# A later and shorter place for the routing of the last batch in a fused attention and mixture-of-experts kernel

## The reference

```python
x = x + tanh(g_xattn[0]) * _L0_xattn_ref(_layernorm(x), ctx_1024, ...)
x = x + tanh(g_ffn[0]) * _L0_ffn_ref(_layernorm(x), ...)

def _L0_ffn_ref(x, w1, b1, w2, b2, wr, br):      # x is 2048 x 256, E = 4, K = 2, H = 1024
    logits = xf @ wr + br
    topk_vals, topk_idx = jax.lax.top_k(logits, K)
    gates = jax.nn.softmax(topk_vals, axis=-1)
    h = jax.nn.gelu(jnp.einsum('nd,edh->enh', xf, w1) + b1[:, None, :], approximate=False)
    y = jnp.einsum('enh,ehd->end', h, w2) + b2[:, None, :]
    ...                                           # gated sum of the two chosen experts
```

## Time and profile before

| | |
|---|---|
| median of 3 runs | 1122.02 us (1119.51 to 1123.55) |
| the profiled execution's own time | 1117.15 us |
| its span in the profile | 1115.6 us |
| PE, DVE, ACT, POOL busy | 96%, 84%, 59%, 48% |
| expert phase in the profile | from about 855 us to the end |

### The profile page before, as it was taken

One profiled execution on the slowest core, in us unless ns is written; L12 is line 12 of the kernel. 1 busy time (PEld: TensorE's weight loads), 2 busy tenths in 40 slices (PEclk: granted clock), 3 DMA queues, 4 the chain that ended last, 5 costly groups with the idle time before them and its releaser, 6 DMA issues.

```text
span 1115.6 us, 22456 instructions
## 1 busy us (share of the span) xinstructions
PE 1067.3 (96%) x7949; PEld 710.8 (64%) x7949; DVE 942.5 (84%) x1764; ACT 655.9 (59%) x1267; POOL 534.1 (48%) x553
## 2 busy tenths in 40 slices
PE   5899999999999999999999999998999988899994
PEld 3556555655555555556555655655546988899994
DVE  7798999898889989898999898878978767676675
ACT  5555556664645765554557656544567675567662
POOL 7433475332436634342565354325851546755561
PEclk9999999999999999999999999999999999999998
DMA  7000010000000000000010000600173423565335
GB/s 205 19 11 11 20 38 11 20 11 11 11 19 26 24 11 10 20 5 26 14 31 15 10 11 11 194 11 35 54 233 140 138 82 130 179 204 173 115 118 176
DMA packets 59188, 72.04 MB, mean 65 GB/s; under 512 B 11579, under 2 KB 52167, under 8 KB 59080
## 3 DMA queue, kind: packets, MB, share of 16 engines
q1 hardware_dynamic: 54840, 61.30, 17.8%
q0 software_dynamic: 3360, 8.53, 2.0%
q10 hardware_dynamic: 880, 0.79, 0.2%
HBM read 54.84 MB, written 16.54 MB: 64 GB/s over the span
## 4 chain that ended last, share of the span: by engine, by line
PE 79%; DVE 13%; issue 3%; ACT 2%; POOL 1%; DMA 1%; SPq 0%; DVEq 0%; POOLq 0%; ACTq 0%
PE pv L1852 16%; PE sc L1836 15%; PE kv L1781 6%; PE kv L1783 5%; PE kv L1782 5%; PE sc L1781 4%; PE sc L1783 4%; PE sc L1782 4%; PE tr L1822 3%; PE mi L1781 3%; PE mi L1782 2%; PE mi L1783 2%; DVE acc L1210 2%; PE mi L1862 2%; DVE prob L1195 1%
## 5 line engine op out<-in xcount | busy, mean ns | idle before, releaser
L953 ACT ACTIVATE prob<-sc 128x1024 f32<-128x1024 f32 x256 | 249.3, 1029 | 198.4 <-PE sc L1836 196.0
L729 POOL TENSOR_TENSOR rot_s<-k_raw,sinb 128x256 f32<-128x256 f32 x128 | 109.7, 857 | 381.2 <-ACT k_raw L898 381.0
L1852 PE MATMUL pv<-prob,val 128*32 128x512 f32 x1984 | 237.8, 597 | 0.7 <-DVE recip L1229 0.7
L1195 DVE TENSOR_SCALAR prob<-prob 128x1024 f32<-128x1024 f32 x256 | 179.8, 715 | 44.6 <-ACT prob L953 42.2
L1836 PE MATMUL sc<-q_hid,w2all 64*128 64x512 f32 x1536 | 213.5, 410 | 1.2 <-DVE w2all L1175 1.2
L1836 PEld LDWEIGHTS sc<-q_hid,w2all 64*128 64x128 f32 x1536 | 135.2, 185 | 101.4 <-issue 54.2
L1210 DVE TENSOR_TENSOR acc<-acc,prob 128x1024 f32<-128x1024 f32 x120 | 177.6, 1501 | 0.0
L733 POOL TENSOR_TENSOR rot_c<-rot_c,rot_s 128x256 f32<-128x256 f32 x128 | 111.0, 867 | 34.1 <-DVE rot_c L1183 19.1
L1852 PEld LDWEIGHTS pv<-prob,val 128*32 128x32 f32 x1984 | 54.8, 109 | 106.1 <-issue 85.3
L1781 PE MATMUL kv<-w2all,acts 128*128 128x512 f32 x248 | 109.8, 443 | 2.2 <-DVE acts L1141 1.3
L1781 PE MATMUL sc<-w2all,q_hid 128*128 x304 | 89.2, 294 | 10.7 <-DVE q_hid L1676 10.3
(11 more groups left out here) (324 smaller groups left out, 2387.7 us busy)
## 6 DMA issues: line engine op xcount, KB each, us to landing
prob<-in_L_ffn_w SPq DMA_DIRECT2D x17, 1024.0 KB
slots_x<-lat_r SPq DMA_DIRECT2D x1, 5016.0 KB, 19.0
rows<-slots_x SPq DMA_DIRECT2D x19, 264.0 KB, 5.6
rows<-in_ctx SPq DMA_DIRECT2D x32, 128.0 KB, 2.2
w_raw<-in_L_xattn_Wq SPq DMA_DIRECT2D x16, 256.0 KB, 3.0
w_raw<-in_L_xattn_Wo SPq DMA_DIRECT2D x64, 64.0 KB
acc<-in_L_ffn_w SPq DMA_DIRECT2D x16, 256.0 KB
acc<-in_L_ffn_w SPq DMA_DIRECT2D x5, 512.0 KB, 5.5
```

The lines of the kernel that those rows point to most:

```text
L729: g.tensor_tensor(rot_s[:].rearrange("p (h a c) -> p h a c", h=4, a=2), kh[:, :, ::-1, :], sinb[:, t].unsqueeze(1).to_broadcast([P, 4, 2, ...
L953: a.activation(prob[:, s % 2, i, :], sc[i][:], ACT.Exp, scale=DH ** -0.5).then_inc(exp_done[i], 1)
L1195: v.tensor_scalar(prob[:, s % 2, i, :], prob[:, s % 2, i, :], EXP_LOW, EXP_HIGH, ALU.max, ALU.min).then_inc(clamped[i], 1)
L1852: last = mm(out_bank(b, p)[g * 32:(g + 1) * 32, :], val[:, u % 2, 2 * c + i, at:at + 32], prob[:, s % 2, i, h * N:(h + 1) * N], start=c == ...
```

## The change

Tiles 6, 7 and 8 are called shared. In their preparation POOL subtracts three chunks instead of four, and DVE subtracts the fourth after block 4 of the tile before (`shared_part`). PE and SP wait for both. The copy of the turned rows on ACT moves from block 6 of tile 2 to block 0 of tile 3. The late batch's work moves: `late_logits` from block 0 to 2 and `rank_gates` from block 1 to 5 of tile 3; the counts on PE from block 4 to 5; the exponential on ACT from tile 3 to tile 4, block 6; `late_spill` from tile 3 block 7 to tile 4 block 5; `late_bases` from tile 4 block 1 to block 6; `late_places` from tile 4 block 5 to 7; `last_gates`, `late_slots` and `records` from tile 4 to tile 5, blocks 5 and 6; `late_owners` from tile 5 block 5 to 7; `tile_biases` from tile 5 block 7 to tile 6 block 7.

```diff
--- before.py
+++ after.py
@@ -332,6 +332,7 @@
         ld_p = [sem(f"ld_p{i}") for i in range(6)]
         neg_mean = sem("neg_mean")
         rows_out = sem("rows_out")
+        shared_low = sem("shared_low")
         p_high = sem("p_high")
         p_low = sem("p_low")
         h_mm = sem("h_mm")
@@ -382,6 +383,7 @@
         SCATTERS_AT.update({3 * STEPS: (14, 18), 3 * STEPS + 1: (18, 21), 3 * STEPS + 2: (21, 24)})
         LATE_SCATTERS = {6: (0, 3), 7: (3, 6), 8: (6, 8)}
         LATE_RANK = 3
+        SHARED = (6, 7, 8)
 
         LOADS_AT = ((0, 1, 2), (3, 4), (5,), (6, 7), (9,), (8,), (), ())
         ROUNDS_AT = ((), (0, 1), (2, 3), (4,), (5,), (6,), (7, 8), (9,))
@@ -622,6 +624,8 @@
                     sp.wait_ge(den_ready, B * PAIRS)
                 else:
                     sp.wait_ge(w_low, job - 2)
+                    if job - 2 in SHARED:
+                        sp.wait_ge(shared_low, SHARED.index(job - 2) + 1)
                 at = job % 2 * KT * 1024
                 raw = wraw[:, 0:KT * 1024] if job == 1 else pall[:, at:at + KT * 1024]
                 sp.dma_start(raw.rearrange("p (k n) -> p k n", k=KT),
@@ -798,7 +802,7 @@
                     pool.wait_ge(wo_mm, B * UNITS * 2)
                 low = g.tensor_tensor(w1_of(job, k, 1)[:, cols], raw_of(job, k)[:, cols],
                                       w1_of(job, k, 0)[:, cols].bitcast(F32), ALU.subtract)
-                if chunk == 3:
+                if chunk == (2 if job in SHARED else 3):
                     low.then_inc(w_low, 1)
 
             def before():
@@ -865,7 +869,7 @@
             attention(before, step)
 
             for job in range(1, JOBS):
-                for chunk in range(4):
+                for chunk in range(3 if job in SHARED else 4):
                     w1_low(job, chunk)
                 for n in range(*LATE_SCATTERS.get(job, (0, 0))):
                     scatter_late(n)
@@ -1093,10 +1097,10 @@
                     o_round(B - 1, PAIRS - 1)
                 if job + 1 < JOBS and m == 3:
                     slots_round(job + 1)
-                if job == LATE_RANK - 1 and m == 6:
+                if job == LATE_RANK and m == 0:
                     x_out(B, 0, tr[:], 0)
                     x_out(B, 1, mi[:], 1)
-                if job == LATE_RANK and m == 6:
+                if job == LATE_RANK + 1 and m == 6:
                     act.wait_ge(f_diff, 2)
                     a.activation(f_tmp[:, EARLY:, :], f_logit[:, EARLY:, :], ACT.Exp).then_inc(f_exp, 1)
                 if job == LATE_RANK + 5 and m == 6:
@@ -1676,6 +1680,12 @@
                 v.scalar_tensor_tensor(dst[:, 1, 0:TS], src, c, dst[:, 0, 0:TS].bitcast(F32),
                                        ALU.subtract, ALU.subtract).then_inc(h_ready, 1)
 
+            def shared_part(job):
+
+                dve.wait_ge(w_high, job * 4)
+                v.tensor_tensor(w1_of(job, 1, 1)[:, 512:1024], raw_of(job, 1)[:, 512:1024],
+                                w1_of(job, 1, 0)[:, 512:1024].bitcast(F32), ALU.subtract).then_inc(shared_low, 1)
+
             def copy_slots(k):
 
                 dve.wait_ge(y_mm, (k + 1) * MT)
@@ -1735,28 +1745,30 @@
                     rows_keep(B - 1)
                 if job == 1 and m in (6, 7):
                     late_norm(EARLY + 2 * (m - 6))
+                if job + 1 in SHARED and m == 4:
+                    shared_part(job + 1)
                 if job == LATE_RANK:
-                    if m == 0:
+                    if m == 2:
                         late_logits()
-                    if m == 1:
+                    if m == 5:
                         rank_gates(EARLY, B * NT)
+                if job == LATE_RANK + 1:
+                    if m == 5:
+                        late_spill()
+                    if m == 6:
+                        late_bases()
                     if m == 7:
-                        late_spill()
-                if job == LATE_RANK + 1:
-                    if m == 1:
-                        late_bases()
+                        late_places()
+                if job == LATE_RANK + 2:
                     if m == 5:
-                        late_places()
+                        last_gates(EARLY, B * NT)
                     if m == 6:
-                        last_gates(EARLY, B * NT)
-                    if m == 7:
                         late_slots()
                         records(EARLY)
-                if job == LATE_RANK + 2:
-                    if m == 5:
+                    if m == 7:
                         late_owners()
-                    if m == 7:
-                        tile_biases(OPEN, JOBS)
+                if job == LATE_RANK + 3 and m == 7:
+                    tile_biases(OPEN, JOBS)
                 if 6 <= job < 14 and m in (5, 6):
                     constant(2 * (job - 6) + m - 5)
                 if job == 14 and m == 7:
@@ -2032,6 +2044,8 @@
                     pe.wait_ge(s_ready, job + 1)
                     if job:
                         pe.wait_ge(w_low, job)
+                    if job in SHARED:
+                        pe.wait_ge(shared_low, SHARED.index(job) + 1)
                 if n == 0:
                     pe.wait_ge(p_low, KT)
                 if n in (1, 2):
@@ -2103,7 +2117,7 @@
                     pe.wait_ge(f_raw, 2 * B + 2)
                     router(B, 0, mi, 0, 0)
                     router(B, 1, mi, 1, 2)
-                if job == LATE_RANK and m == 4:
+                if job == LATE_RANK and m == 5:
                     pe.wait_ge(f_lout, 2 * B + 2)
                     late_counts()
                 if job == 14 and m == 4:
```

## The result

The changed kernel takes 1116.26 us (median of 9 runs, 1114.49 to 1118.54), the kernel before 1122.02 in the same comparison: a ratio of 0.9947, interval 0.9936 to 0.9959. The profiled executions differ by less than that: 1115.35 (span 1113.6) against 1117.15 (span 1115.6), 1.8 us.

A forecast was written before the change was run, and what follows sets the result against it. PE, busy 96% of the span, was taken as the bound, with only six waits of 8.84 us to win. The terms summed to −1.1 us, 1116.05 against the profiled execution, 1120.9 as median; range 1116.5 to 1124.5.

The forecast's parts named there:

- the last of the sum: Whole kernel: 1.1 us gained on the profiled 1117.15 gives 1116.05; with its 4.9 us distance to the median, 1120.9.
- the held signal: Tiles 5 to 7: beside five POOL transfers in a row, ACT starts a gelu 2.6 us after PE's matmul; cause unknown.
- Copies, −0.86: End of tile 2: block 7's gelu no longer waits for PE's turning, so PE's wait goes, −0.86 us.
- Tile 3 to 4, −2.02: Boundary of tiles 3 and 4: without table loads and `late_spill` in tile 3, PE's wait goes, −2.02 us.
- Tile 4 to 5, +1.9: Boundary of tiles 4 and 5: Exp, table loads and `late_places` meet, chain held by a POOL subtraction, +1.9 us.
- Tile 5 to 6, −1.5: Boundary of tiles 5 and 6: `tile_biases` gone, shared subtraction and late chain earlier than PE's start, −1.5 us.
- the signal's new place in tile 6, +1.2: Blocks 1 to 3 of tile 6: ACT's late gelu moves here from the boundary, costing 0 to 2.3, taken as +1.2 us.
- Tile 6 to 7, +0.5: Boundary of tiles 6 and 7: POOL's transfers start later, so turn 7 is held longer, +0.5 us (0 to 1.5).
- Tile 7 to 8, −0.3: Boundary of tiles 7 and 8: POOL has one chunk less and transfers come earlier, −0.3 of 0.73 us.
- Rival (a): Tiles 4 to 7: PE's lead swallows more, chain misses POOL's op, held signal costs nothing; −3.7 us, 1118.3; chance 0.20.
- Rival (c): Tiles 6 and 7: slower, POOL late with tile 7's weights behind transfers awaiting the route; +4.1 us, 1126.1; chance 0.10.
- The chance of "faster", 0.17: Whole kernel: chance of a measurement faster beyond 0.3% (3.4 us), from two thirds of rival (a) plus 0.04 for scatter.

The follow-up runs named there:

- e1: The kernel before, unchanged, run again: 1112.13 us, ratio 0.9997.
- e14: The kernel before with POOL's indirect transfers never more than two in a row, in a comparison where before took 1121.32 us: 1116.08 us, ratio 0.9952.
- e2: The kernel before with only the two copies of turned rows moved to block 0 of tile 3: 1110.99 us, ratio 0.9989.
- e10: The kernel before with the copies moved and the late gates' Exp in block 4 of tile 3 instead of block 6: 1109.17 us, ratio 0.9972.
- e11: The kernel before with the copies moved and the late gates' Exp in block 5 of tile 3: 1109.13 us, ratio 0.9977.
- e13: The changed kernel with the late gates' Exp in block 4 of tile 4 instead of block 6; before took 1121.32 us: 1115.32 us, ratio 0.9945.
- e17: The change without DVE's shared subtraction (copies and ranking moved), in a comparison where before took 1121.96 us: 1117.02 us, ratio 0.9945.
- e3: The kernel before with only the late batch's ranking chain moved; copies and POOL's four subtractions stay: 1114.77 us, ratio 1.0026.
- e18: The kernel before with copies moved and Exp in block 4 of tile 3, where before took 1121.96 us: 1117.41 us, ratio 0.9960.
- e9: The kernel before with all eight late scatters behind tile 6's weights, so ten indirect transfers in a row: 1118.08 us (two executions), ratio 1.0058.
- e7: The kernel before with POOL's runs of transfers cut by subtractions, two at most in a row, at the lower level: 1115.22 us, ratio 1.0028.
- e5: The changed kernel, unchanged, run again at the lower level: 1113.76 us, ratio 1.0013.

## Why the prediction was wrong

Medians in us, and what the upper level adds:

| kernel | lower | upper | added |
|---|---|---|---|
| before | 1112.2 | 1122.0 | 9.8 |
| before, transfers spread | 1115.2, 1115.4 | 1116.1 | 0.8 |
| copies, Exp in block 4 | 1109.2 | 1117.4 | 8.2 |
| copies and ranking | 1113.4, 1115.8 | 1117.0 | 1.2 to 3.7 |
| changed | 1113.8 | 1116.3 | 2.5 |

**The step that failed** is the last of the sum: "That one ran 4.9 us under the median of the runs, 1122.02, and I forecast the median: 1120.9." I took the 4.9 us as something that stands beside the change. The upper level adds 9.8 us to the kernel before and 2.5 to the changed one; the difference of 7.3, less the 1.4 to 1.6 that the change costs at the lower level, is the 5.8 measured. The profiled execution of before shows only 5.6 of the 9.8 (its stretches 5|6 to 7|8 less those of e1: 2.34, 2.31 and 0.99). So the held signal was priced from an execution that had little more than half of the level's cost. A part of the rest goes with PE's clock: the profiled execution had 0.992, and three others of before at the upper level with 0.991 to 0.993 took 1119.00 to 1120.56 us, against 1121.96 to 1123.30 at 0.988. From these numbers I estimate 2 to 3 of the 4.9 us. The changed kernel's nine executions had 0.989 to 0.993, with a median of 0.992, so some of its gain may be clock that it does not lose; no run separates this. What the remainder is stays open: e14 brings the median from 1121.32 to 1116.08 by the order of transfers alone, but no trace of an execution at 1122 us shows where its time goes.

Against the two profiled executions the terms stand so:

- Copies, −0.86: 2|3 gives 1.31, and 1.17 alone (e2). Right in kind, a third too small; the wait is gone.
- Tile 3 to 4, −2.02: 2.08. Right.
- Tile 4 to 5, +1.9: 1.87. Right, held instruction included: one of `late_places` took 1.19 us for 0.2 (DVE's timeline of the changed kernel, of before).

```profile
922.29 0.17 DVE L1593 TENSOR_TENSOR lat_r<-r_keep,lat_r 128x16 f32<-128x16 f32 x1
922.49 1.19 DVE L1594 TENSOR_SCALAR lat_r<-lat_r 128x16 f32<-128x16 f32 x1
923.71 0.17 DVE L1595 SCALAR_TENSOR_TENSOR lat_r<-lat_r 128x16 f32<-128x16 f32 x1
```

  That the wait in 3|4 goes with the Exp and not with the chain, e10 and e11 show; in 4|5 the Exp accounts for 0.55 only (e13). The prediction left open which it was.
- Tile 5 to 6, −1.5, and the signal's new place in tile 6, +1.2: −0.3 together; 5|6 is 0.21 longer. PE's wait at tile 6's start fell from 2.26 to 0.82, and the late gelu is in block 3 of tile 6, both as forecast. ACT went on at 942.18, before the fifth transfer ended at 942.48, and not 1.1 us after it.
- Tile 6 to 7, +0.5: wrong sign, −0.42. PE's wait of 2.07 became 0.87, although turn 7's signals are still late by 2.4 us.
- Tile 7 to 8, −0.3: −0.24. Sum −2.0 against −1.1.
- Six waits of PE in tiles 2 to 8 were counted. There is a seventh, of 0.74 at 883.51, at tile 2's first block; it is 0.75 in the changed kernel and no part of the difference.

Rival (a) came nearest in number (1118.3), but the trace does not show what it said: the chain met POOL's subtraction, and the held signal still cost PE 0.40 and 0.32 us in tile 6. What makes the later run so much cheaper is shown only in part. Turn 6 has one late signal of 1.45 us where before had 1.13 and 2.62, turn 7 has 2.38 for 2.64, turn 8 0.42 for 1.23. That is not all, since e17, without the shared quarter, has signals late by 2.90 and 2.89 and still takes 1117.0. In 5|6 the changed kernel is as slow at the lower level (14.92) as at the upper (14.90), for two different delays: there the hold of DVE, here the late signal, without the hold. In 6|7 and 7|8 the upper level still adds 1.8 us.

Rival (c) named the right place for the loss at the lower level, tile 6, and the wrong mechanism: I wrote that POOL has no subtraction to hold DVE with while it waits for the route. It has three right behind (four in e3), without gaps, and they hold `choose`. At the lower level 5|6 is 2.57 and 6|7 0.85 longer than before, with the 2.08 us hold in the first, and the change is slower there.

The chance of "faster", 0.17, rested on a scatter of runs around one level. The profiled execution's distance of 4.9 us from a median of three runs that span 4 us was the sign that something varied from run to run; the held signal was the one delay for which I had found no cause in the trace, and was the first to suspect.

## What to carry to other kernels

When the profiled execution lies further from the median than the runs lie from each other, ask which of its delays could be longer in the others, and forecast for both cases: what a change does to that delay can outweigh all that it does in the trace. Compare the granted clock of the profiled execution with that of the others too. Work given to GpSimd behind a wait comes out of it in a row without gaps, and then keeps small VectorE instructions out for most of the row; one subtraction less made the hold 2.08 us instead of 3.30. A function on ScalarE that costs two table loads is worth trying in other blocks: two blocks earlier took 1.7 us off PE's wait here.

## What the hardware did that I had not expected

- A signal of TensorE's last matmul reached ScalarE up to 2.90 us late (e17) after GpSimd had begun the third of its indirect transfers in a row, in all profiles at the upper level whose kernel has such runs (before, changed, e13, e17, e18), and in none at the lower level, even with ten in a row (e9). Why is open.
- The same unchanged kernel stood at 1112.2 us in four comparisons and at 1121.3 to 1122.0 in three. What sets the level stays open; at equal granted clock the two are still some 8 to 10 us apart. The order of GpSimd's transfers (e14) and the later place of the ranking, with the copies (e17), change what it costs.
- TensorE fell to the lower of its clock levels for 3.4 us in some executions around or just behind a wait of 1.7 to 3.1 us, and not in others of the same kernel with the same wait; it cost 1.3 us of a stretch (e14 against e7).
- A VectorE instruction on 16 elements a partition was kept out for 3.30 us beside a row of four GpSimd subtractions (e3), and for 2.08 beside a row of three (e5).
